# A two-layer vision tower in float32 on one core: probabilities divided as rows in layer 0, two products of layer 1 regrouped, four engine orders written out

## The reference

```python
h = concat([cls_tok, cls_token, patches(x) @ W.T + b]) + pos_embed   # (32, 38, 256)
# layer 0
q, k, v = heads(ln(h) @ Wq.T), heads(ln(h) @ Wk.T), heads(ln(h) @ Wv.T)   # 16 heads of 16
p = softmax(mask(rope(q) @ rope(k).T * 0.25))        # causal
h = h + (p @ v) @ Wo.T
h = h + moe(ln(h))     # 8 experts, top 2 by a gate: w_out[e] @ (w_in[e] @ x), no nonlinearity
# layer 1
a = ln(h); q, k = a @ Wq.T + bq, a @ Wk.T + bk       # 16 heads, no mask
# 8 shared values of 16 numbers, each head mixes its 8 results by a softmax over scores
# that depend on a (Wqv, Ws); then Wf, a residual, and a two-product MLP with relu (Wr1, Wr2)
h = h + mixed_attention(a)
y = gelu(ln(h) @ ternary(W_fc).T); h = h + ln(y) @ ternary(W_proj).T
```

## Time and profile before

| | us |
|---|---|
| runs of the kernel before | 561.04, 561.39, 558.50 |
| their median | 561.04 |
| the profiled execution | 560.32 |
| its span, first to last instruction | 558.5 |
| TensorE busy | 506.9 (91%) |
| DVE busy | 375.7 (67%) |
| ACT busy | 272.9 (49%) |
| POOL busy | 190.3 (34%) |

### The profile page before, as it was taken

The page is one execution under the profiler, slowest core; times in us unless marked ns, Lnnn a source line. Parts: engine busy times, 40 slices in busy tenths (PEclk is TensorE's granted clock), DMA queues, the critical chain, the costliest instruction groups (busy, mean ns, idle before and its releaser), DMA issues.

```text
span 558.5 us, 12004 instructions
## 1 busy us (share of the span) xinstructions
PE 506.9 (91%) x3850; PEld 424.5 (76%) x3850; DVE 375.7 (67%) x943; ACT 272.9 (49%) x634; POOL 190.3 (34%) x257
## 2 busy tenths in 40 slices
PE   2969999999999887789999999999999989889996
PEld 2758878878787665567778888888888778668885
DVE  4554464555466667565997878878878787648874
ACT  3021213232331363547668777777777886434332
POOL 3320321322323311375463364364363311222230
PEclk9788899999999999999999999999999999979999
DMA  8741333243140500000000000000000000000000
GB/s 318 285 175 38 141 150 120 80 175 150 31 169 0 179 2 2 0 1 2 1 1 2 2 0 0 0 0 0 0 0 0 2 0 1 2 9 21 21 18 22
DMA packets 8685, 29.60 MB, mean 53 GB/s; under 512 B 1936, under 2 KB 3152, under 8 KB 6352
## 3 DMA queue, kind: packets, MB, share of 16 engines
q1 hardware_dynamic: 8656, 29.23, 14.4%
HBM read 27.98 MB, written 1.25 MB: 52 GB/s over the span
## 4 chain that ended last, share of the span: by engine, by line
PE 42%; DVE 5%; issue 5%; ACT 3%; POOL 1%; DVEq 1%; POOLq 0%; ACTq 0%
PE score L2051 6%; PE tb L1803 3%; PE score L1868 3%; PE bz L2081 3%; PE tb L1805 3%; PE tb L1804 3%; PE bank L1805 3%; PE bank L1804 3%; PE bank L1803 3%; PE tb L1886 2%; PE bz L2063 2%; PE bz L1817 2%; PE bz L1803 1%; DVE we_h L1433 1%; PE tb L1817 1%
## 5 line engine op out<-in xcount | busy, mean ns | idle before, releaser
L378 POOL TENSOR_TENSOR h<-h,scaled 114x256 f32 (+1 forms) x88 | 69.0, 784 | 49.3 <-ACT scaled L681 42.7
L330 POOL TENSOR_TENSOR small<-small,half 114x1 f32<-114x1 f32 x44 | 25.7, 584 | 139.4 <-DVE small L964 139.3
L547 ACT ACTIVATE p_exp<-sc,cst 114x608 f32<-114x608 f32 x66 | 48.1, 794 | 24.7 <-DVE sc L1045 24.7
L1915 PE MATMUL bz<-ebuf 128*128 128x256 f32 x256 | 58.9, 383 | 0.0
L1915 PEld LDWEIGHTS bz<-ebuf 128*128 128x128 f32 x256 | 47.8, 192 | 6.0 <-issue 0.2
L1886 PE MATMUL tb<-cst,p_exp 114*114 114x114 f32 x352 | 44.0, 266 | 9.0 <-ACT p_exp L547 3.4
L555 ACT ACTIVATE pt<-tb 114x456 f32<-114x456 f32 x66 | 34.6, 556 | 35.3 <-PE tb L1886 35.3
L2051 PE MATMUL score<-v,pt 114*114 114x137 f32 x352 | 48.9, 282 | 0.3 <-ACT o L648 0.3
L1886 PEld LDWEIGHTS tb<-cst,p_exp 114*114 114x114 f32 x352 | 35.2, 134 | 18.2 <-ACT pt L555 6.7
L681 ACT ACTIVATE scaled<-bank,gl 114x256 f32<-114x256 f32 x88 | 39.0, 473 | 17.3 <-DVE gl L1249 5.9
L2051 PEld LDWEIGHTS score<-v,pt 114*114 114x114 f32 x352 | 44.1, 178 | 2.1 <-issue 0.4
(11 more groups left out here) (216 smaller groups left out, 1338.7 us busy)
## 6 DMA issues: line engine op xcount, KB each, us to landing
ebuf<-in_w_in SPq DMA_DIRECT2D x8, 1024.0 KB, 4.8
ebuf<-in_w_out SPq DMA_DIRECT2D x8, 1024.0 KB, 6.8
x_raw<-in_x_tiles SPq DMA_DIRECT2D x11, 342.0 KB, 3.0
out<-h SPq DMA_DIRECT2D x10, 114.0 KB
raw<-in_w_a SPq DMA_DIRECT2D x4, 256.0 KB, 4.2
ebuf<-in_fc SPq DMA_DIRECT2D x1, 1024.0 KB, 5.6
ebuf<-in_proj SPq DMA_DIRECT2D x1, 1024.0 KB, 7.6
raw<-in_w_a SPq DMA_DIRECT2D x2, 384.0 KB, 5.2
```

The costliest lines, as they stand in the source:

```text
L378: gp.tensor_tensor(h[0:R, t, :], h[0:R, t, :], scaled[0:R, e % 4, :], ALU.add).then_inc(moe_acc, 1)
L547: act.activation(p_exp[0:R, :, b * S:(b + 1) * S], sc[0:R], ACT.Exp, bias=cst[0:R, CB + b:CB + b + 1], scale=SCALE).then_inc(exps, 1)
L1915: last = pe.matmul(bz[:, m * D:(m + 1) * D], ebuf[:, 0, c * D + m * P:c * D + (m + 1) * P], ebuf[:, 1, c * D:(c + 1) * D], start=(c == 0), ...
```

## The change

- Layer 0's softmax: ACT makes one exponential into `sc` in place (`a2_exp`); DVE sums it over each head's 38 keys, takes the reciprocal of 16 sums a row and multiplies (`a2_norm`); ACT then writes the three wide copies with a factor of 1 or 0 (`a2_wide`, `inside`). The product with `hsum`, the reciprocal of 228 columns (`a2_recip`) and the multiplication (`a2_o` on DVE) go; `a2_o` on ACT and `a2_lo` read the PV bank, and `scores` waits for `oT_lo`.
- Layer 1: query with values (392 columns) is one product, key with the mix's part (272 columns) the other; the weights are loaded in that order (three DMAs in place of one); ACT moves the rows in two instructions; the table sums come before the transposes. The gate is four matmuls, two of them with high and low weights side by side, summed by DVE.
- Experts: the product runs chunk by chunk over both halves of the output, and its weights are loaded in halves.
- Beginning: dummy matmuls (`warm`) ahead of and behind the first patch product; the preparation of layer 1's weights (`prep_products`, `prep_qv`) comes later.
- SP: the ternary weights are fetched before the last x tile, and their size sums come earlier in ACT's order.
- The loops of C and D are written out on all four engines, in new orders; D's tiles 0 to 9 start between the last tiles of C. The orders of tiles 8 to 10 of A change too. The loop of A stays, with a changed step.

The diff, cut to its core (of the orders the first lines of TensorE's, and its end):

```diff
-C_QK, C_V, C_G, C_F, C_R1, C_R2, C_END = np.cumsum([0, DC * 2 * D, DC * W2, DC * E, DC * D, DC * 2 * D, 4 * D]).tolist()
+WQ = D + VW + RK
+W4 = 2 * D + W2
+C_QK, C_G, C_F, C_R1, C_R2, C_END = np.cumsum([0, DC * W4, DC * E, DC * D, DC * 2 * D, 4 * D]).tolist()
...
-            def load_expert(e):
-                sp.dma_start(ebuf[:, 0, :], w_in[e]).then_inc(expert_in, 16)
-                sp.dma_start(ebuf[:, 1, :], w_out[e]).then_inc(expert_in, 16)
+            def load_expert(e, half_):
+                part = slice(half_ * HC * D // 2, (half_ + 1) * HC * D // 2)
+                sp.dma_start(ebuf[:, 0, part], w_in[e][:, part]).then_inc(expert_in[half_], 16)
+                sp.dma_start(ebuf[:, 1, part], w_out[e][:, part]).then_inc(expert_in[half_], 16)
...
+            mine = raw[:, C_QK:C_G].rearrange("p (c n) -> p c n", c=DC)
+            qk_in = w_c[:, 0:DC * 2 * D].rearrange("p (c n) -> p c n", c=DC)
+            v_in = w_c[:, DC * 2 * D:C_G].rearrange("p (c n) -> p c n", c=DC)
+            sp.dma_start(mine[:, :, 0:D], qk_in[:, :, 0:D]).then_inc(wc_in, 16)
+            sp.dma_start(mine[:, :, D:WQ], v_in[:, :, 0:VW + RK]).then_inc(wc_in, 16)
+            sp.dma_start(mine[:, :, WQ:WQ + D], qk_in[:, :, D:2 * D]).then_inc(wc_in, 16)
+            sp.dma_start(raw[:, C_G:C_F], w_c[:, C_G:C_F]).then_inc(wc_in, 16)
...
                 load_x(t + 1)
+                sp.wait_ge(half_combined, t)
+                load_expert(t, 0)
                 sp.wait_ge(combined, t)
-                load_expert(t)
+                load_expert(t, 1)
             load_x(E + 1)
-            load_x(E + 2)
             sp.wait_ge(combined, E)
             sp.dma_start(ebuf[:, 0, :], fc).then_inc(fc_in, 16)
             sp.dma_start(ebuf[:, 1, :], proj).then_inc(proj_in, 16)
+            load_x(E + 2)
...
+            def a2_exp(n):
+                act.wait_ge(shifted, 2 * n + 2)
+                act.activation(sc[0:R], sc[0:R], ACT.Exp, scale=SCALE).then_inc(dense, 1)
+
+            def a2_wide(n, batches=range(G)):
+                act.wait_ge(scaled_rows, n + 1)
+                since(act, pt_mm, 4 * n)
+                for b in batches:
+                    act.activation(p_exp[0:R, :, b * S:(b + 1) * S], sc[0:R], ACT.Copy,
+                                   scale=inside[0:R, b:b + 1]).then_inc(exps, 1)
             def a2_o(t):
-                act.wait_ge(o_ready, t + 1)
+                act.wait_ge(pv0_mm, t + 1)
                 since(act, wo_mm, t)
-                act.activation(xth[1][:], y2[:], ACT.Copy).then_inc(oT_hi, 1)
+                act.activation(xth[1][:], two(score[:, 0, 0:2 * R]), ACT.Copy).then_inc(oT_hi, 1)
...
+            tern_sum(0)
             a1_x(8)
-            softmax_exp(7, (0, 1, 2))
+            a2_exp(7)
+            a2_wide(7, (0, 1, 2))
             a1_pt(7, (0, 2))
+            a1_q(8, (0,))
+            a2_o(7)
...
-            def a2_recip(t):
-                dve.wait_ge(pv0_mm, t + 1)
-                V.reciprocal(rinv0, score[:, 0, 2 * R:4 * R]).then_inc(rinv0_ready, 1)
-
-            def a2_o(t):
-                dve.wait_ge(rinv0_ready, t + 1)
-                since(dve, oT_lo, t)
-                V.tensor_tensor(y2[:], two(score[:, 0, 0:2 * R]), two(rinv0), ALU.mult).then_inc(o_ready, 1)
+            def a2_norm(n, k):
+                if k == 0:
+                    dve.wait_ge(dense, n + 1)
+                    V.tensor_reduce(psum_rows[0:R, 0], sc[0:R], AX, ALU.add).then_inc(summed, 1)
+                elif k == 1:
+                    dve.wait_ge(summed, n + 1)
+                    V.reciprocal(psum_rows[0:R, 1], psum_rows[0:R, 0]).then_inc(inverted, 1)
+                else:
+                    dve.wait_ge(inverted, n + 1)
+                    V.tensor_tensor(sc[0:R], sc[0:R], psum_rows[0:R, 1].unsqueeze(2).broadcast_to([R, H, S]),
+                                    ALU.mult).then_inc(scaled_rows, 1)
 
             def a2_lo(t):
                 dve.wait_ge(oT_hi, t + 1)
-                V.tensor_tensor(xtl[1][:], y2[:], xth[1][:].bitcast(F32), ALU.subtract).then_inc(oT_lo, 1)
+                V.tensor_tensor(xtl[1][:], two(score[:, 0, 0:2 * R]), xth[1][:].bitcast(F32), ALU.subtract).then_inc(oT_lo, 1)
...
-                for e in range(2):
-                    for j in range(4):
-                        last = pe.matmul(score[32 * j:32 * j + 32, 0, 2 * R:4 * R], hsum[0:R, e * 2 * HD:(e + 1) * 2 * HD],
-                                         pt[0:R, place(2 * j + e):place(2 * j + e) + HQ + 1:HQ, :], start=(e == 0), stop=(e == 1))
                 last.then_inc(pv0_mm, 1)
...
+            def combine(e, chunks):
+
+                if 0 in chunks:
+                    pe.wait_ge(expert_in[0], 32 * e + 32)
                     since(pe, we_lo, e)
+                if HC // 2 in chunks:
+                    pe.wait_ge(expert_in[1], 32 * e + 32)
                 for c in chunks:
-                    last = pe.matmul(bz[:, m * D:(m + 1) * D], ebuf[:, 0, c * D + m * P:c * D + (m + 1) * P],
-                                     ebuf[:, 1, c * D:(c + 1) * D], start=(c == 0), stop=(c == HC - 1))
-                if m == DC - 1 and HC - 1 in chunks:
+                    for m in range(DC):
+                        last = pe.matmul(bz[:, m * D:(m + 1) * D], ebuf[:, 0, c * D + m * P:c * D + (m + 1) * P],
+                                         ebuf[:, 1, c * D:(c + 1) * D], start=(c == 0 and m == 0),
+                                         stop=(c == HC - 1 and m == DC - 1))
+                if HC // 2 - 1 in chunks:
+                    last.then_inc(half_combined, 1)
+                if HC - 1 in chunks:
                     last.then_inc(combined, 1)
 
-            pe.wait_ge(init, 7)
+            def warm(n):
+                for i in range(n):
+                    pe.matmul(bz[:, 0:P], ones[:], ones[:], start=True, stop=True)
+
+            pe.wait_ge(init, 2)
+            warm(12)
+            pe.wait_ge(init, 5)
             a1_patch(0)
+            warm(14)
             pe.wait_ge(cst_in, 16)
             a1_x(0)
             pe.wait_ge(wa_lo, 5)
             a1_qk(0)
             a1_v(0)
-            combine(0, 0, (0, 1, 2, 3))
+            combine(0, (0, 1))
...
             def a_step(t):
                 scores(t - 1, True)
                 a1_x(t)
-                combine(t, 0)
+                combine(t, (0, 1, 2, 3))
                 a1_qk(t)
                 a1_v(t)
+                combine(t, (4, 5))
                 a1_turn(t - 1)
-                combine(t, 1)
+                combine(t, (6, 7))
                 a2_pv(t - 1)
                 a1_qT(t)
                 a1_kT(t)
                 a1_patch(t + 1)
                 a2_wo(t - 1)
 
...
-                product(bk[0][0:R, 256:256 + E], xth[0], xtl[0], wc, C_G, E, (0, E)).then_inc(gate_mm, 1)
+                for c in range(DC):
+                    pe.matmul(bk[0][0:R, 256:256 + 2 * E].rearrange("p (a e) -> p a e", a=2), xth[0][:, c, :],
+                              wc[:, :, C_G + c * E:C_G + (c + 1) * E], start=(c == 0), stop=False)
+                    last = pe.matmul(bk[0][0:R, 256:256 + E], xtl[0][:, c, :], wc[:, 0, C_G + c * E:C_G + (c + 1) * E],
+                                     start=False, stop=(c == DC - 1))
+                last.then_inc(gate_mm, 1)
...
             def c2_qk(t):
                 pe.wait_ge(t2["lo"], t + 1)
-                product(tb[1][0:R, :], xth[1], xtl[1], wc, C_QK, 2 * D, (0, 2 * D)).then_inc(qk1_mm, 1)
+                since(pe, pt_odd, 2 * (t + T))
+                product(tb[1][0:R, 0:WQ], xth[1], xtl[1], wc, C_QK, W4, (0, WQ)).then_inc(qk1_mm, 1)
 
             def c2_v(t):
-                pe.wait_ge(q_ready, 2 * (t + T) + 2)
-                product(tb[0][0:R, 2 * R:2 * R + W2], xth[1], xtl[1], wc, C_V, W2, (0, W2)).then_inc(v1_mm, 1)
+                pe.wait_ge(t2["lo"], t + 1)
+                product(tb[0][0:R, 0:D + H], xth[1], xtl[1], wc, C_QK, W4, (WQ, W4)).then_inc(v1_mm, 1)
 
             def c2_qT(t):
-                pe.wait_ge(qk1_out, t + 1)
+                pe.wait_ge(qk1_out, 2 * t + 2)
+                pe.wait_ge(v1_ready, 2 * t + 2)
                 turned(tb[0][:, 0:2 * R], qk_rows[:, 0:D]).then_inc(qkT1_mm, 1)
 
             def c2_kT(t):
-                pe.wait_ge(qk1_out, t + 1)
+                pe.wait_ge(qk1_out, 2 * t + 2)
+                pe.wait_ge(v1_ready, 2 * t + 1)
                 turned(tb[1][:, 0:2 * R], qk_rows[:, D:2 * D]).then_inc(qkT1_mm, 1)
 
...
             scores(7, True)
             a1_x(8)
+            a1_patch(9)
             a1_qk(8)
-            a1_patch(9)
             a1_turn(7, (0, 1, 2, 3))
+            a1_v(8)
             a1_qT(8)
             a1_kT(8)
             a2_pv(7)
             a1_x(9)
-            a1_v(8)
...
+            d2_turn(0, (0, 1))
+            proj_bias()
+            d1_fc(2, (0,))
+            proj_sums()
+            d1_fc(2, (1,))
             c3_x(9)
-            proj_bias()
```

(59 more changed lines are left out.)

1862 lines of the change are left out of this document (1242 added, 620 removed).

## The result

The changed kernel takes 566.9 us (median of 8 runs, 563.4 to 571.4) where the kernel before, on the same chip, took 560.5 (8 runs, 556.7 to 562.5): a ratio of 1.0125, interval 1.0094 to 1.0157. **It is slower by 1.25%, 6 to 7 us; forecast was 26.5 us faster.** The profiled execution took 567.27 us, span 565.5, so the spans differ by 7.0.

A forecast was written before the change was run, and what follows sets the result against it. PE's own work was taken to bound the steady parts, chains through DVE and ACT the start, passage and end. Terms -8.4 - 9 + 3 + 2 - 4.1 - 2 - 8 = -26.5 took 560.3 to 533.8 us, range 516 to 551.

The forecast's parts named there:

- Part 1, rows divided: Layer 0's loop: hsum product gone, longer softmax chain covered; 1.4 us saved per tile, -8.4 us over six tiles.
- Part 2, the beginning: Kernel start: dummies bring the higher clock sooner, preparation moves later, scores(1) at 48.8; -9 us, bounds -4 and -12.
- query/key runs at 0.24 a matmul, not at twice that: Beginning: after 14 more dummies the first query/key product runs at the higher clock; some 3.5 us won by first expert product.
- Part 3, the passage: Layer 0's tiles 7 to 10: longer chain shows, no expert product behind the scores; +3 us, bounds -3 and +7.
- One fall costs 3.4 us of clock: Passage: idle turns of 2 to 5 us bring one fall to the lower clock, +2 us.
- rival B: Passage: all four turns bring a clock fall, some 3 us each; +10, 544 us; chance 0.15.
- Part 4, layer 1: Layer 1: merged products and smaller gate -4.1 us; new order -2, bounds -6 and +3.
- -4.1, all on PE: Layer 1, 11 tiles: merged products take 1.86 instead of 2.04 us, the gate 0.2 less; -4.1 us.
- new PE idle in layer 1: Layer 1: a sign named beforehand that would show the forecast wrong; no size given.
- I give the new order -2: From turn 10 into layer 1: the written order recovers PE idle time; -2 us, bounds -6 and +3.
- Part 5, the end: Kernel end: last stage's tiles fill PE's idle and low clock around tile 10's residual chain; -8 us, bounds -3 and -11.
- Rival D: Layer 0's loop: divided rows come late and waits bring the lower clock; slower, up to 592 us; chance 0.04.

The follow-up runs named there:

- x11: x10 without the two groups of 12 and 14 dummy products in the beginning; 543.9 us, ratio 0.9722.
- x10: x7 with the loops of layer 1 and of the last stage written out as well; 540.9 us, ratio 0.9664.
- x2: The changed kernel with dummy matmuls in the passage, ahead of patch 9 and of turns 8, 9 and 10; 560.65 us, ratio 1.0018.
- x13: x2 with the last stage's second product alternating between two banks; 548.3 us, ratio 0.9782.
- x6: x5 with x2's dummy products in the passage; 548.1 us, ratio 0.9804.
- x14: x12 with dummy products in front of turns 7 to 10 and of scores 8 to 10; 551.5 us, ratio 0.9849.
- x9: x2 with layer 1's separate products of before (512 and 152 columns) in the change's written order; 563.4 us, ratio 1.006.
- x7: The kernel before with only the new beginning, the new layer 0 loop and the gate of four matmuls; 542.9 us, ratio 0.9711.
- x1: The changed kernel with the old orders and loops behind the ternary sums, merged products kept; 577.5 us, ratio 1.0323.
- x5: x1 with the two separate products (512 and 152 columns) in place of the merged ones; 559.5 us, ratio 1.0004.
- x15: x10 with two banks for the last stage's second product; 541.6 us, ratio 0.9679.
- x16: The changed kernel with two banks for the last stage's second product, nothing else; 559.6 us, ratio 0.9991.
- x8: The kernel before with its loops of layer 1 and of the last stage written out, nothing else; 556.8 us, ratio 0.9941.
- x12: x10 with the rows of tiles 7 to 10 divided the new way, in the old order of the passage; 557.9 us, ratio 0.9977.

## Why the prediction was wrong

**Part 1, rows divided: right.** The period is 111.3/6 = 18.5 on average and 18.4 in the steady part, forecast 18.3; the loop won 8.0 of 8.4. The chain behind the scores goes from 4.7 to 7.4 us (109.4 to 116.75), forecast 7.8, and is covered: PE's turn at 117.69 comes after it.

**Part 2, the beginning: right in kind, 2.4 short.** Scores(1) comes at 51.3, not 48.8 (50.0 to 53.5 in the other profiles with this beginning). The first patch matmuls stand 0.12 apart, as forecast:

```profile
3.75 1.83 PE L2490 MATMUL bz<-ones 128*128 128x128 f32 x12
6.48 0.34 PE L2369 MATMUL bank<-wa,xs 128*114 128x256 f32 x1 [0.89 <-DVE wa L1238]
...
6.89 0.28 PE L2369 MATMUL bank<-wa,xs 128*114 128x256 f32 x1
7.01 0.28 PE L2370 MATMUL bank<-wa,xs 128*114 128x256 f32 x1
```

x11 shows the dummies' share in x10: 3.9 at scores(0), against 1.5 + 2. In the profile of the change the second of these terms didn't come in full, though ("query/key runs at 0.24 a matmul, not at twice that"): it stands 0.42 to 0.43 apart, the lower clock in spite of the 14 dummies, and 0.23 apart in x2, x10 and x13:

```profile
14.69 0.63 PE L2370 MATMUL bank<-wa,xth 128*114 128x512 f32 x1
15.11 0.63 PE L2371 MATMUL bank<-wa,xtl 128*114 128x512 f32 x1
```

Scores(0) comes at 22.0, in x2 at 20.8. Where the rest of the 2.4 went no run tells.

**Part 3, the passage: the step that failed is "One fall costs 3.4 us of clock in the stretch from 480, of which PE would have used 2. I add one".** The waits of 2 to 5 us at the turns were forecast and came at three of four (2.3, 3.5 and 4.4), and so did the idle ahead of patch 9 (3.2, forecast 2.9). Each of the four is followed by matmuls at the lower clock. The clock in them is 8.0 us (x2, 6.2 by the medians), 10.5 in x6 (11.4) and 8.6 in the old order (x14, 6.4): three to six times the term, in the change, by the lengths, four times. So the price of one fall, 2 us, was about right, and the count of one was not. I had the pair of slow transposes behind 2.05 of idle at 38.43 and set against it the clock of 1.00 in the stretch where PE waited 1.7; but 1.7 is less than any wait that I forecast, so that row said nothing of them. The Trainium skill ("TensorE: Matmul & The Clock Gate", HAM oscillation) tells of a kernel whose matmuls start at the lower clock behind every wait for data. Taken to these turns it gives rival B's term, and the trace agrees at the three turns that waited. The chain's share was 4.8 in the new order against +3, inside the bound of 7; in an order not made for it, it is 8 to 10 (x14).

**Part 4, layer 1.** The step that failed is "-4.1, all on PE". The spacings came as forecast, 0.18 and 0.13:

```profile
343.29 0.34 PE L2370 MATMUL tb<-wc,xth 128*114 128x392 f32 x1
343.47 0.34 PE L2371 MATMUL tb<-wc,xtl 128*114 128x392 f32 x1
...
344.77 0.29 PE L2370 MATMUL tb<-wc,xth 128*114 128x272 f32 x1
344.90 0.29 PE L2371 MATMUL tb<-wc,xtl 128*114 128x272 f32 x1
```

But the time saved on PE was mostly not time saved. Some 2.0 of it are the products and 2.2 the gate (11 tiles at 0.18 and 0.2). x2 against x9 tests only the products: 3.0 us at most, of which 0.8 lies in layer 1. The gate gave nothing that shows (20.97 a tile in x7 with it, 20.96 before). In the change PE is idle for 3.3 us between 300 and 420, where the kernel before had 40.00 in each 40: the "new PE idle in layer 1" that the prediction named as a sign of being wrong. The pair of expert products that I named as cover for the longer chain lies ahead of the query transpose in x1 too, and PE waits there all the same; without the written order the merging costs 18 us (x1 against x5).
"I give the new order -2" can't be told apart from the order's share in part 5. Together, with 3.0 for merging, the written loops and the bank's wait set aside, 319.0 - 310.3 + 3.0 + 3.5 - 11.3 = +3.9 is left, where -2 and -8 were forecast. The waits for qvs, 3.3 us in seven, are part of it, and so is one of 3.1 for the GELU at 478.15, which the kernel before doesn't have; what else no run tells.

**Part 5, the end: the step that failed is "The new order lays the last stage's tiles there; DVE, with 10.54 busy of 20, has room".** Room on the engine was not the limit. Each second product waits until the output of the tile before is out, because both use one bank, and in the written order that output stands in DVE's list, and on GpSimd, behind other tiles' work: layer 1's last tiles for the first waits, the last stage's own tiles for the later ones (2.0 us at 558.59, when layer 1 is over). In the old order the wait was nil (x15). It costs 11.3 us (x2 to x13 and the change to x16, by the rest). The Trainium skill ("Perfetto Trace Analysis", Matmuls) wants independent matmul groups to rotate through banks; x13 and x15 show that here it is worth 11 us in one order and nothing in the other.

Writing the loops out, which I cost at nothing, gained 3.5 us, nearly all of it in the last stage (x8): I had read PE's 40.00 of 40 in layer 1's loop for both loops, and the last stage's had 19.55 of 20.

**The sum.** With the clock's term at its measured 8 the forecast would have been 539.8, still far off. The largest error is the end: 11.3 for the bank's wait, for which the prediction had nothing, and the orders of parts 4 and 5 at +3.9 instead of -10. Rival D had the sign, but not the place: the loop's chain was never exposed. No rival had a wait for the bank.

## What to carry over

A chain made longer by 3 us is free only where an engine has work beside it, so look at each place where it runs, and price the clock behind each exposed wait: here four waits of 2.3 to 4.4 us brought 8 us of clock on top, and useless matmuls bought them back. An instruction taken off an engine is time won only where that engine's own work bounds the stretch afterwards. Before tiles of the next stage are laid between those of the last, list for each product which bank it writes and which output must be out first, since the output now queues behind other tiles' work. A bundle of changes is best tried in parts: two of these five, with the loops written out and the new gate, give 540.9 us where all five give 566.9.

## What the runs showed that I had not expected

Adding 53 dummy products to the passage made the kernel 6 us faster (x2), and 55 made x12 6 us faster (x14). A loop's head costs where its body is short: 0.4 us for each turn of 6.1, nothing measurable where the turn takes 20.95 (x8). And the same edit, the longer chain at four tiles, cost 17 us with the clock left to fall and 8 to 10 with it held.
